# Maximum taken one tick late, ring of five banks, state reduction in one group, GpSimd's product with the next scan and the scan's carries on GpSimd

## What is computed

```python
# layer 0
y = leaky_relu(conv3x3(x, w1) + b1); y = leaky_relu(conv3x3(y, w2) + b2)
x, z = split(seq @ in_proj_w)                     # 128 inner channels each
x = silu(causal_conv4(x)); dt, Bm, Cm = split(x @ x_proj_w)       # 4, 16, 16
delta = softplus(dt @ dt_proj_w + dt_proj_b)
h = exp(delta * A) * h + (delta * x) * Bm         # per channel 16 states, over 4096 steps
y = (h . Cm) + x * D;  out = (y * silu(z)) @ out_proj_w
# layer 1, hw = 4096
attn_c = softmax(xc @ xc.T)                       # 64 x 64;  xc = w_cam x
attn_s = softmax(q.T @ k)                         # 4096 x 4096;  q, k: 32 channels
out = x + w_bn @ concat(attn_c @ x, v @ attn_s.T)
```

## Time and profile before

| | |
|---|---|
| median of three runs | 9002.96 us (8994.49 to 9007.99) |
| the profiled execution | 9007.69 us; span from first to last instruction 9005.9 us |
| TensorE busy (PE) | 8085.0 us, 90% of the span, mean granted clock 0.969 |
| VectorE (DVE) | 7220.5 us, 80% |
| ScalarE (ACT) | 6245.7 us, 69% |
| GpSimd (POOL) | 3213.1 us, 36% |
| DMA | 1530 MB, mean 170 GB/s, the 16 engines' share 0.7 |

### The profile page before, as it was taken

How to read it: one execution, slowest core, us unless ns; L and a number is a source line. 1 busy time by engine, 2 the same in 40 slices (tenths; PEclk the granted TensorE clock), 3 DMA queues, 4 the chain that set the end, 5 groups by cost and what they waited for, 6 DMA issues and landing times. The chain is left out here.

```text
span 9005.9 us, 135283 instructions
## 1 busy us (share of the span) xinstructions
PE 8085.0 (90%) x38865; PEld 2124.9 (24%) x39494; DVE 7220.5 (80%) x10982; ACT 6245.7 (69%) x12374; POOL 3213.1 (36%) x2343
## 2 busy tenths in 40 slices
PE   8962499999999999989999999989999999999999
PEld 2210122222222222222222222222222222222222
DVE  1238989888898888888888889888888988888721
ACT  1124577777777777777777777777777777777754
POOL 0015444343443434333434434333434434333300
PEclk9986699999999999999999999999999999999999
DMA  8758877767677767767776767767777777677500
GB/s 126 117 107 208 205 186 184 184 176 187 179 185 180 192 175 188 183 171 191 178 190 177 191 180 186 181 172 187 183 185 182 188 178 192 175 180 182 148 27 10
DMA packets 868046, 1530.07 MB, mean 170 GB/s; under 512 B 403336, under 2 KB 436944, under 8 KB 867280
## 3 DMA queue, kind: packets, MB, share of 16 engines
q1 hardware_dynamic: 864208, 1520.77, 68.4%
q10 hardware_dynamic: 3072, 0.40, 0.0%
HBM read 1326.69 MB, written 176.95 MB: 167 GB/s over the span
## 5 line engine op out<-in xcount | busy, mean ns | idle before, releaser
L1251 POOL TENSOR_TENSOR hst<-hst,cbc 128x512 f32<-128x512 f32 x2048 | 2844.7, 1390 | 4630.5 <-ACT carry L1007 4005.7
L996 ACT ACTIVATE pr<-bank 128x512 f32<-128x512 f32 x4096 | 2224.9, 597 | 1051.5 <-PE bank L880 950.2
L1144 DVE TENSOR_TENSOR_SCAN hst<-dA,carry,bank 128x512 f32<-128x512 f32 x1792 | 2294.0, 1280 | 64.4 <-DVE bank L1134 0.3
L889 PE MATMUL bank<-pr,vt 128*64 128x512 f32 x8192 | 2212.4, 618 | 0.0
L1086 DVE CUSTOM_DVE_ANT_0 gains<-bank,gains 128x512 f32<-128x512 f32 x2048 | 1406.2, 687 | 855.1 <-ACT gains L944 829.9
L1134 DVE TENSOR_TENSOR bank<-lanes,bbc 128x512 f32<-128x512 f32 x2048 | 1680.3, 820 | 74.2 <-DMA lanes<-spread_d 31.4
L1002 ACT ACTIVATE dA<-lanes,small 128x512 f32<-128x512 f32 x2048 | 1489.4, 727 | 235.6 <-DMA lanes<-spread_d 146.5
L880 PE MATMUL bank<-t2q,t2k 128*128 128x512 bf16 x4096 | 1554.6, 380 | 108.5 <-issue 66.5
L829 PE MATMUL bank<-s1kx,s1q 128*128 128x512 bf16 x4096 | 1337.5, 389 | 286.1 <-DVE mxp L1086 248.2
L878 PE MATMUL bank<-s1q,s1k 128*128 128x512 bf16 x3467 | 1329.4, 383 | 136.0 <-ACT pr L996 135.5
L944 ACT ACTIVATE gains<-bank 128x512 f32<-128x512 f32 x2048 | 1235.6, 603 | 187.0 <-PE bank L829 183.0
(11 more groups left out here) (116 smaller groups left out, 5804.9 us busy)
## 6 DMA issues: line engine op xcount, KB each, us to landing
lanes<-spread_d SPq DMA_DIRECT2D x2048, 512.0 KB, 5.3
seqt<-seq_d SPq DMA_DIRECT2D x256, 128.0 KB, 4.4
spread_d<-dsp SPq DMA_DIRECT2D x128, 256.0 KB, 2.0
spread_d<-usp SPq DMA_DIRECT2D x128, 256.0 KB, 2.0
bbc<-bc_d SPq DMA_DIRECT2D x128, 256.0 KB, 3.3
cbc<-bc_d SPq DMA_DIRECT2D x128, 256.0 KB, 3.8
xpad<-in_x SPq DMA_DIRECT2D x64, 256.0 KB, 6.7
ypad<-ypad SPq DMA_DIRECT2D x128, 128.0 KB, 4.1
```

Of the source, the lines that this page charges most:

```text
L889: mm = nc.tensor.matmul(ACC[CH * h:CH * (h + 1), :], vt[:, t, :], pr[:, T % PRING, h, :], start=t == 0, stop=t == KT - 1)
L996: nc.scalar.activation(pr[:, T % PRING, h, :], bank_of(("S", T, h))[:], ACT.Exp).then_inc(S["p_full"], 1)
L1144: nc.vector.tensor_tensor_scan(hst[:, T % HRING, :], dA[:, T % 2, :], DBU[:], carry[:, g:g + 1] if sl % CHUNKS else 0.0, ALU.mult, ALU.add ...
L1251: nc.gpsimd.tensor_tensor(h, h, cbc[:, (T - 1) // GROUPS % 2, :], ALU.mult).then_inc(S["hc_in"], 1)
```

## The change

- The maximum of tick T-1 is computed in tick T: TensorE's order in a tick is dif, S, S, max of T-1, PV of T-1, SUM, small uses. ScalarE takes Relu(dif) first in its tick, VectorE takes the max right after the scan.
- The ring has five banks. `YPS` is gone; the state reduction is now a use of the ring ("y") in tick r = 2 of the next chunk, 16 matmuls in one piece. `hst` grows from 8 to 24 slots so that a chunk's states stay until then. `ysb` moves from r = 4 to the start of r = 3.
- GpSimd's product of slot T-1 also waits for VectorE's product of T (`dbu_in`), so that it begins with scan T.
- The carry copy moves from ScalarE to GpSimd, ahead of its product.
- To make room, `bcs` lies in unused partitions of `rest`, and `rinv` in `dens` (with one more wait). The load of the search's keys moves one tick.

```diff
...
-SEARCH_LOAD = [SEARCH - KT + 8 * (p + 1) for p in range(QUARTERS - 1)] + [GROUPS]
+SEARCH_LOAD = [SEARCH - KT + 8 * (p + 1) + 1 for p in range(QUARTERS - 1)] + [GROUPS]
 PRING = 4
-HRING = 8
-BATCH = 4
+HALVES = GROUPS // 2
+HRING = GROUPS + HALVES
 SLOTS = 4
 AHEAD = 3
...
     k = T % GROUPS
     return k % BLOCKS * GPB + k // BLOCKS
+
+
+def slot_of(T):
+
+    k = T % GROUPS
+    return k if k >= HALVES or T // GROUPS % 2 == 0 else k + GROUPS
 class Span:
...
     def small_uses(self, T):
         ev = []
-        found = self.searches(T)
+        found, last = self.searches(T), self.searches(T - 1)
         if found:
-            t = (T - SEARCH) % KT
-            ev += [("dif", found, t), ("max", found, t)]
+            ev.append(("dif", found, (T - SEARCH) % KT))
+        if last:
+            ev.append(("max", last, (T - 1 - SEARCH) % KT))
         turned = self.quarter_at(T, TURN)
         if turned:
             ev.append(("turn", turned))
...
         for name in {0: ("xin", "z"), 6: ("dt",), 10: ("BC",)}.get(r, ()):
             if self.chunk(sl + 1):
                 ev.append((name, sl + 1))
-        name = {7: "out", 12: "xv", 14: "en"}.get(r)
+        name = {2: "y", 7: "out", 12: "xv", 14: "en"}.get(r)
         if name and self.chunk(sl - 1):
             ev.append((name, sl - 1))
         return ev
     def plan(self, T):
-        uses, plan = self.small_uses(T), []
+        uses = self.small_uses(T)
+        plan = [e for e in uses if e[0] == "dif"]
         if self.attends(T):
             plan += [("S", T, 0), ("S", T, 1)]
+        plan += [e for e in uses if e[0] == "max"]
         if self.attends(T - 1):
             plan.append(("PV", T - 1))
-        plan += uses[0:2]
-        b = T // BATCH - 1
         if T % 2 == 0 and self.attends(T - 1):
             plan.append(("SUM", T // 2 - 1))
-        if T % BATCH == BATCH - 1 and self.scans(BATCH * b):
-            plan.append(("Y", b))
-        return plan + uses[2:]
-
-
-SIGNAL_OF = {"PV": "pv", "SUM": "den", "Y": "y_mm"}
-DVE_USES = ("max", "turn", "mix", "res", "en")
-RING = 4
+        return plan + [e for e in uses if e[0] not in ("dif", "max")]
+
+
+SIGNAL_OF = {"PV": "pv", "SUM": "den"}
+DVE_USES = ("max", "turn", "mix", "res", "en", "y")
+RING = 5
...
     x1_d, parts_d, kx_d, vt_d, spread_d, bc_d, den_d, rin_d = scratch
-    RB, (DBU, ACC, DEN, YPS) = banks[0:RING], banks[RING:]
-    AUX = RB[0]
+    RB, (DBU, ACC, DEN) = banks[0:RING], banks[RING:]
+    AUX, AUX2 = RB[0], RB[1]
...
-        bcs = sb("bcs", [2 * D_STATE, CHUNK])
...
+        bcs = rest[0:2 * D_STATE, 0:CHUNK]
...
-        rinv = sb("rinv", [P, CHUNK])
...
-                    for at, n in ((4, "y_in"), (4, "y2_in"), (8, "st_x1"), (8, "kd_in"), (9, "head_in"),
+                    for at, n in ((4, "y2_in"), (8, "st_x1"), (8, "kd_in"), (9, "head_in"),
...
-                for n, offset in (("max_in", TURN - 2), ("nm3_in", TURN), ("nm_row", TURN + 1), ("acc_in", MAIN + KT),
+                for n, offset in (("max_in", TURN - 1), ("nm3_in", TURN), ("nm_row", TURN + 1), ("acc_in", MAIN + KT),
...
+                        elif kind == "y":
+                            wait(pe, "hc_in", GROUPS * (c + 1) - 1)
+                            for gl in range(GPB):
+                                for j in range(BLOCKS):
+                                    mm = nc.tensor.matmul(
+                                        bank[BLOCK * j:BLOCK * (j + 1), :],
+                                        cst[:, C_SUM + BLOCK * gl:C_SUM + BLOCK * (gl + 1)],
+                                        hst[:, slot_of(GROUPS * c + BLOCKS * gl + j), :],
+                                        start=gl == 0, stop=gl == GPB - 1, tile_position=(0, BLOCK * j))
...
-                    def reduce_states(b):
-
-                        gl = b % GPB
-                        if gl == 0:
-                            wait(pe, "y_in", b // GPB - 1)
-                        wait(pe, "hc_in", BLOCKS * b + BLOCKS - 1)
-                        for j in range(BLOCKS):
-                            mm = nc.tensor.matmul(YPS[BLOCK * j:BLOCK * (j + 1), :],
-                                                  cst[:, C_SUM + BLOCK * gl:C_SUM + BLOCK * (gl + 1)],
-                                                  hst[:, (BLOCKS * b + j) % HRING, :],
-                                                  start=gl == 0, stop=gl == GPB - 1, tile_position=(0, BLOCK * j))
-                        mm.then_inc(S["y_mm"], 1)
...
-                            elif e[0] == "Y":
-                                reduce_states(e[1])
...
-                            dst, src = bcs[:], bank[0:2 * D_STATE, :]
+                            dst, src = bcs, bank[0:2 * D_STATE, :]
...
                     for T in range(first, last):
                         sl, r = T // GROUPS, T % GROUPS
+                        near = [e for e in sched.small_uses(T) if e[0] == "dif"]
+                        for e in near:
+                            small_use(e)
                         if sched.attends(T):
                             wait(act, "pv", (T - PRING,))
                             wait(act, "den", ((T - PRING) // 2,))
...
                             g = group_of(T + 1)
                             nc.scalar.activation(dA[:, (T + 1) % 2, :], lanes[:, (T + 1) % SLOTS, 0, :], ACT.Exp,
                                                  scale=amat[:, g:g + 1]).then_inc(S["da_in"], 1)
-                        if sched.carries(T - 1):
-                            wait(act, "scan", T - 1)
-                            g = group_of(T - 1)
-                            nc.scalar.copy(carry[:, g:g + 1],
-                                           hst[:, (T - 1) % HRING, CHUNK - 1:CHUNK]).then_inc(S["carried"], 1)
-                        for e in sched.small_uses(T):
+                        for e in sched.small_uses(T)[len(near):]:
                             small_use(e)
...
                         if done:
                             wait(act, "st_den", sched.before(done), 16)
                             wait(act, "den", ((T - 1) // 2 - 1,))
+                            taken(act, ("res", sched.before(done)))
                             nc.scalar.copy(dens[:], DEN[:]).then_inc(S["den_in"], 1)
...
-                            wait(act, "y_in", c - 2)
+                            taken(act, ("y", c - 2))
...
                     def small_use(e):
                         kind, c = e[0], e[1]
-                        if kind not in DVE_USES:
+                        if kind not in DVE_USES or kind == "y":
                             return
                         full_wait(dve, e)
                         bank = bank_of(e)
...
                         sl, r = T // GROUPS, T % GROUPS
                         ev = sched.small_uses(T)
                         c = sl - 1
-                        if sched.chunk(c) and r == 4:
-                            wait(dve, "y_mm", (GPB * (c + 1) - 1,))
+                        if sched.chunk(c) and r == 3:
+                            full_wait(dve, ("y", c))
                             full_wait(dve, ("out", c - 1))
-                            nc.vector.scalar_tensor_tensor(out=ysb[:], in0=u[:, c % 2, :], scalar=dskip, in1=YPS[:],
-                                                           op0=ALU.mult, op1=ALU.add).then_inc(S["y_in"], 1)
+                            nc.vector.scalar_tensor_tensor(out=ysb[:], in0=u[:, c % 2, :], scalar=dskip, in1=bank_of(("y", c))[:],
+                                                           op0=ALU.mult, op1=ALU.add).then_inc(S["dve_took"], 1)
...
                                 dve.wait_ge(S["dbu_in"], due("dbu_in", T))
                             if due("da_in", T):
                                 dve.wait_ge(S["da_in"], due("da_in", T))
-                            wait(dve, "y_mm", ((T - HRING) // BATCH,))
+                            wait(dve, "carried", T - GROUPS)
+                            full_wait(dve, ("y", sl - 1 if T % GROUPS >= HALVES else sl - 2))
                             nc.vector.tensor_tensor_scan(
-                                hst[:, T % HRING, :], dA[:, T % 2, :], DBU[:],
+                                hst[:, slot_of(T), :], dA[:, T % 2, :], DBU[:],
                                 carry[:, g:g + 1] if sl % CHUNKS else 0.0, ALU.mult, ALU.add).then_inc(S["scan"], 1)
+                        for e in ev:
+                            if e[0] == "max":
+                                small_use(e)
                         c = sl + 1
                         if sched.chunk(c):
...
                         for e in ev:
-                            small_use(e)
+                            if e[0] != "max":
+                                small_use(e)
                         a = sched.channel(T, GROUPS)
...
                                 wait(pool, "ld_c", sl, 16)
                             if due("scan", T - 1):
```

(11 more changed lines are left out.)

9 lines of the change are left out of this document (5 added, 4 removed).

## The result

The kernel with the change takes 8544.82 us (median of 4 runs, 8542.00 to 8548.87), the kernel before 9004.57 in the same comparison: a ratio of 0.9492 with a 95% interval of 0.9475 to 0.9508. It is 5% faster, and 25 us above the predicted 8520. The profiled execution took 8545.51 us with a span of 8543.7, against 9007.69 before: 462 us less.

What follows compares the result with a forecast made beforehand. TensorE was taken as the bound, with handshake stalls. Main stage 3.66 instead of 3.90 us a tick (453 us less), first scan stage 25 less and tail 8 less gave 8521 from 9007.69, stated as 8520; range 8390 to 8850.

Steps and rivals of the forecast that it cites:

- TensorE's tick without stalls: Main stage: a TensorE tick without stalls falls from 3.61 to 3.54 us, by fewer steps from bf16 to fp32.
- Stalls of TensorE: Main stage, us a tick: 0.03 for VectorE's lag, 0.075 for table loads, 0.015 for channel attention; 0.29 before.
- the rest: Added waits for bcs and rinv, the search load moving with max, hst's 24 slots: together nothing.
- Y's wait: VectorE's ysb at tick 3 stands about 4 us each chunk for the Y matmuls, just about within VectorE's spare time.
- VectorE's contention: With GpSimd's product beside the scan, about 370 us, 3 us a chunk, leave VectorE; worth nothing on the path.
- rival C: VectorE bounds, as GpSimd's product does not stay under the scan: 3.78 us a tick, about 8765 us; chance 0.16.
- The carry: The copy moved from ScalarE to GpSimd is hidden under the max: nothing, between -0.05 and +0.05 us a tick.
- The lock in the first stage: First scan stage: the next two-input instruction would wait out GpSimd's last 0.1 us, 16 us in all; sum 8537 with it.
- The signs: Wrong if Y's wait is much over 4 us, TensorE idles 6%, GpSimd's copy exceeds 1 us or VectorE awaits dA.
- A: The Y burst stalls everybody and TensorE pays its 4 us again: slower, about 9070 us; chance 0.07.
- B: TensorE's stalls stay, coming from ScalarE's and VectorE's own lumps and not the ring: 8830 us; chance 0.11.
- D: No TensorE stall is left, VectorE's 53 + 4 us fitting its chunk: 3.55 us a tick, 8315 us; chance 0.10.

Runs made afterwards that it cites:

- before + ring: Kernel before with five banks, state reduction as one use at r = 2, hst of 24 slots and ysb at r = 3: 8942.51 us, ratio 0.9932.

## Why the prediction was right

By its steps:

- *TensorE's tick without stalls*, 3.54: measured 3.50. The ticks are as predicted (3.40 and 2.41 against 3.41 and 2.42). Y in one piece takes 3.55 and not 4.0: back to back its four groups of 8 come every 0.89 us, where a lone one took 1.00. The small uses are 6.0 again. (The prediction's ground for that was loose: it took 0.12 us of overlap from a row that gives 0.08. But the distances between starts in the chunk above add up to 6.1.) A chunk is 8 x 5.81 + 3.55 + 6.0 = 56.0 us, where the prediction had 56.6. This term was 0.036 too high, 67 us.
- *Stalls of TensorE*, 0.12: measured 3.67 - 3.50 = 0.17. The term of 0.12 was 0.05 too low, 94 us, and part by part it went otherwise than its total says. The exponential's share was right (0.075 predicted, 152.3 / 1889 = 0.081). The two shares of VectorE, 0.03 for its lag and 0.015 for the channel attention, 85 us, did not come: TensorE's list has no wait for the maximum. The four stops of 9 to 13 us, 45 us together, were left out, though the kernel before has them too. The 17.6 us of waits for `gains` were not foreseen. And the late key load costs 57 us by the run with the load a tick earlier. The prediction put it down under "the rest ... nothing". That step failed: it looked at the load's own move by one tick and not at the reader that the skew had moved to the front of its tick, and not at the one entry of the list that had not moved. Some 50 us of stalls have no row. The 67 us too many of the first term and the 94 too few of this one cancel but for 27, which is nearly the 25 us by which the forecast is off. That closeness is luck.
- *Waits that go*: `gains` gone; none for `mxp` in TensorE's list (under 60 predicted); those for `pr`, "some 100" us at r = 10, are 152.3 us, at r = 10 indeed (5040.63, 1.30 us ahead of the second S).
- *Y's wait*: 345 us in 113 times, 3 us each instead of 4, since Y is shorter and VectorE is ready only 4.2 us into the tick (5009.91 to 5014.07) instead of 3.2 to 3.6. That VectorE could spare it was right: moving it away gained nothing.
- *VectorE's contention*, about 370 us: 430 less busy. L1132's mean came to 738, not 700, since GpSimd's product of `ysb` has no such wait and still collides, as at 5023.30: from 3000 to 4000 us, 17 of 270 products take over 0.75 us, all of them beside it, and they hold nearly all of the excess. The whole mean above 0.69 is (0.738 - 0.690) x 1889 = 91 us. So the product gave 136 us and not 227; that the total came out higher is mostly due to groups which the prediction did not count, among them the multiplication of `accs` (1602 to 692 ns) and the maximum (686 to 667).
- *Where I was wrong in kind*: "on the path this is worth nothing while TensorE bounds". It would be true if 3 us of VectorE's time lay well inside what it has to spare. They do not. In the runs where GpSimd's product begins late, VectorE is busy 56 to 57 us a chunk (before + ring 56.8 of 61.7, after with the carry on ScalarE 56.0 and 2.9 of standing of 61.5). With 2 to 5 us left, lumps of its work reach TensorE: the carry, which frees nothing on TensorE, is worth 330 us. That the same holds back the ring (62 us with Y in one piece in the kernel before, 158 for the bank alone in the change) is argued and not shown, since the two edits differ, and the skew gained 190 us with a VectorE as busy (56.2 of 61.0). The forecast held because the product did stay under the scan; had it not, the time would not be rival C's 8765 but 8875 (carry on ScalarE) or 9427 (no wait). C took VectorE's chunk at 56 us, as before. The skew puts the maximum right behind the scan and two-input work right behind that, so a product of GpSimd's that starts with the maximum costs more than it did in the old order: 63.7 us. No run has the old order with GpSimd's copy and no wait, so this last is argued too.
- *The carry*, "nothing, -0.05 to +0.05 a tick": GpSimd's copy is 0.18 us for the most part (0.26 in the mean) and hidden, as said. But ScalarE's copy was the releaser of GpSimd's product, which the row itself showed (`[0.79 <-ACT carry L1007]`), and moving it is what lets the product start with the scan. This step was mis-sized by 330 us; it did not show in the sum, since the sum took for granted that the product lies under the scan, for which the copy's move turned out to be needed.
- *First stage*, -25: measured -30; L1132's mean there is 121.22 / 160 = 758 ns (121.22 us busy in the window 600 to 1123) against 871. *Tail*, -8: measured -4.
- *The lock in the first stage.* Above 0.69 there are still (0.758 - 0.690) x 160 = 11 us in the products of that window. They are not the last 0.1 us behind the scan: ten products that stand beside a product of GpSimd's, nine times that of `ysb`, take 1.36 to 1.78 us and hold nearly all of it. Right behind a scan (the second line below) VectorE's product starts 0.11 us after the scan's end and takes 0.70, and in the kernel before it does the same where nothing of GpSimd's is near (823.43, 0.11 and 0.70).

```profile
810.04 1.28 DVE L1143 TENSOR_TENSOR_SCAN hst<-dA,carry,bank 128x512 f32<-128x512 f32 x1
811.43 0.70 DVE L1132 TENSOR_TENSOR bank<-lanes,bbc 128x512 f32<-128x512 f32 x1
...
838.39 1.77 DVE L1132 TENSOR_TENSOR bank<-lanes,bbc 128x512 f32<-128x512 f32 x1
```

The prediction drew on the Trainium skill, page "SBUF — State Buffer", section "SBUF: two separate sides", for an estimate of 16 us and a sum of 8537. Such a wait behind the scan does not show on the product, and on `u` (L1172) it is 0.72 us instead of 0.67; the lock shows where two such instructions really overlap, as at 838.39. The stage gained 30 us, so the sum of 8537, though nearer to 8545, was nearer by accident.
- *The signs.* Y's wait, TensorE's idle share (3.7%), the DMA share (0.77) and GpSimd's copy (0.26 us in the mean, at most 0.98) came out on the right side. One sign of being wrong was met, VectorE's wait for dA (45.6 us in 103 times), but it does not mean what the prediction said: ScalarE is busy in 5425.8 of 6936 us and is not the bound. The sign was drawn too tight.

*The rivals.* A (the burst stalls everybody) is refuted by the time, and covering the `ysb` wait gains nothing. B (stalls stay) is refuted by the change itself; with the ring alone the waits for the maximum do stay (8943). C's mechanism is real and larger than I had it. D (8315) is refuted too: even without the table loads 8479 is left. (Its "53 + 4" is 57 and not "no more than" 56.6; VectorE's own chunk came to 6068.23 / 118 = 51.4.)

## What to carry to other kernels

When an engine that is not the bound has under a tenth of its time to spare, price its work by what it leaves for handshakes and not at nothing: here VectorE's 51.5 us a chunk grew to 56.0, of some 60, and the whole took 330 us more. Look for who releases an instruction that blocks another engine; a copy of 0.2 us in a busy queue can decide where a 1.3 us instruction lands. And after moving a consumer forward in its tick, check the due time of each of its loads, the last of a list too.

## What the runs showed of the hardware

VectorE instructions with two SBUF inputs and GpSimd's product exclude each other nearly in full (VectorE's length goes from 0.75 to 1.65 us and from 0.69 to 1.68), and GpSimd's copy of one column, 0.18 us alone, took 0.64 when it came second. The scan, with one SBUF input and one from a bank, took 1.28 beside a product of 1.27 and 1.28 alone. A stop of TensorE of 2.73 us was followed by under 4 us in which bf16 matmuls started 0.43 instead of 0.22 us apart; windows of 10 us there read a granted clock of 0.89 and 0.94. Four fp32 groups of 8 matmuls in four column tiles came 0.89 us apart, against 1.00 for one between other work.
